# Who builds the transposed one-hot of a chunk: GpSimd in 16 pieces between its gathers, in place of VectorE in one operation

## What is computed

```python
edge_index_t = jnp.stack([src, dst], axis=1)
xn = _layernorm(x, axis=-1)
x = x + _L0_gnn_ref(xn, edge_index_t, ...) + _L0_mix_ref(xn[None], ...)[0]
x = x + _L0_ffn_ref(_layernorm(x, axis=-1)[None], ...)[0]
```

```python
qe = q[:, c, :]; ke = k[:, r, :]; ve = v[:, r, :]
sim = jnp.einsum('hed,hed->eh', qe, ke) * scale
m = jax.ops.segment_max(sim, c, num_segments=bs)
p = jnp.exp(sim - m[c])
s = jax.ops.segment_sum(p, c, num_segments=bs)
attn = p / s[c]
agg = jax.ops.segment_sum(out_e, c, num_segments=bs)   # out_e = attn * ve
```

## Time and profile before

| | |
|---|---|
| time, median of 3 runs | 1684.04 us (1683.97 to 1684.6) |
| profiled execution | 1672.81 us, span 1671.1 us |
| busy: TensorE, VectorE, ScalarE, GpSimd | 1051.0, 1016.4, 420.2, 573.4 us |
| attention rounds | from about 270 to 1293 us of the span |

### The profile page before, as it was taken

One profiled execution on the slowest core, in us unless ns is written; L12 is line 12 of the kernel. 1 busy time (PEld: TensorE's weight loads), 2 busy tenths in 40 slices (PEclk: granted clock), 3 DMA queues, 4 the chain that ended last, 5 costly groups with the idle time before them and its releaser, 6 DMA issues. The chain is left out here.

```text
span 1671.1 us, 20984 instructions
## 1 busy us (share of the span) xinstructions
PE 1051.0 (63%) x4059; PEld 682.8 (41%) x4060; DVE 1016.4 (61%) x2562; ACT 420.2 (25%) x1228; POOL 573.4 (34%) x651
## 2 busy tenths in 40 slices
PE   0389563655656565565665656655656870899996
PEld 0245341433334343343433333333433570557574
DVE  5369866766666566666666666666677740234343
ACT  1212252222222222222222222222223240121211
POOL 1224336233433333334444433433330007323231
PEclk9789776777776667777677766777677955899998
DMA  4531324244444444444444444444430234143420
GB/s 141 83 126 62 98 58 125 86 132 116 122 127 119 114 114 114 114 119 122 129 130 129 127 130 117 122 128 118 114 103 1 88 127 124 45 151 102 155 95 11
DMA packets 85034, 181.19 MB, mean 108 GB/s; under 512 B 13797, under 2 KB 49819, under 8 KB 84999
## 3 DMA queue, kind: packets, MB, share of 16 engines
q0 software_dynamic: 39744, 120.22, 26.0%
q1 hardware_dynamic: 45255, 60.56, 11.6%
HBM read 158.49 MB, written 24.89 MB: 110 GB/s over the span
## 5 line engine op out<-in xcount | busy, mean ns | idle before, releaser
L1104 PE MATMUL at_pa<-at_pv,at_hot 128*125 128x264 f32 x832 | 321.2, 532 | 226.8 <-DVE agg L978 152.1
L1104 PEld LDWEIGHTS at_pa<-at_pv,at_hot 128*125 128x125 f32 x832 | 193.1, 253 | 327.3 <-issue 250.6
L850 POOL DMA_INDIRECT slot<-kv_d,idx x192 | 184.0, 958 | 295.0 <-ACT idx L859 242.9
L1047 PE MATMUL at_pq<-q,at_hotT 125*128 x1248 | 234.3, 332 | 78.3 <-DVE at_prod L986 55.0
L850 POOL DMA_INDIRECT at_slot<-kv_d,idx x192 | 184.1, 959 | 289.4 <-ACT idx L859 237.0
L1047 PEld LDWEIGHTS at_pq<-q,at_hotT 125*128 125x128 bf16 x1248 | 143.3, 115 | 164.3 <-issue 110.0
L978 DVE TENSOR_TENSOR agg<-agg,at_pa 125x264 f32 x416 | 176.7, 425 | 37.0 <-remote 10.2
L1021 DVE TENSOR_TENSOR at_pv<-at_slot,at_pp 128x528 f32<-128x528 f32 x104 | 71.8, 701 | 125.0 <-remote 74.7
L1021 DVE TENSOR_TENSOR at_pv<-slot,at_pp 128x528 f32<-128x528 f32 x104 | 71.8, 701 | 118.8 <-remote 74.8
L907 DVE TENSOR_REDUCE at_sc<-at_prod 128x16 f32<-128x512 f32 x208 | 139.4, 671 | 0.0
L865 ACT ACTIVATE at_habs<-iota_w,nloc_e 128x125 f32<-128x125 f32 x416 | 131.1, 386 | 0.2 <-issue 0.2
(11 more groups left out here) (297 smaller groups left out, 1462.7 us busy)
## 6 DMA issues: line engine op xcount, KB each, us to landing
slot<-in_w SPq DMA_DIRECT2D x16, 1024.0 KB, 6.3
at_locrow<-loc_d SPq DMA_DIRECT2D x26, 500.0 KB
slots_d<-slot SPq DMA_DIRECT2D x7, 516.0 KB
kv_d<-vst SPq DMA_DIRECT2D x25, 128.9 KB
base<-in_x SPq DMA_DIRECT2D x5, 625.0 KB
kv_d<-kst SPq DMA_DIRECT2D x25, 125.0 KB
x_d<-base SPq DMA_DIRECT2D x5, 625.0 KB
out<-base SPq DMA_DIRECT2D x5, 625.0 KB
```

Of the source, the lines that this page charges most:

```text
L850: pool.indirect_dma_start(slot[par][:, u, :], None, m.kv_d, bass.IndirectOffsetOnAxis(ap=m.idx[:, par, u:u + 1].bitcast(U32), axis=0)).the ...
L1047: mm = pe.matmul(pq[j % 2][:, (u % 2) * D:(u % 2 + 1) * D], hotT[:, u, :], at(m.q3, window)[:, part, :], start=(part == 0), stop=(part == 2))
L1104: mm = pe.matmul(pa[u % 4][:, 0:H * VW], hot[:, u % 8, :], pv[:, u % 4, :, :].rearrange("p h c -> p (h c)"), start=True, stop=True)
```

## The change

VectorE's `turned_hots` is gone. GpSimd makes the same tile step by step, 125x128 each, with `turned_hot(u)`: all 16 steps ahead of the first loop for chunks 0 and 1; in the loop four steps (AHEAD) before the first gather of the chunk and then one behind each of the first 12 gathers. `hotT_made` now counts steps and no longer chunks, so SyncE waits for 16 times n, and TensorE waits once for each pair of steps and no longer once for a chunk.

```diff
@@ block.sync
-                        wait(sp, S.hotT_made, n)
+                        wait(sp, S.hotT_made, U * n)
@@ block.gpsimd
+                def turned_hot(u):
+                    pool.tensor_scalar(hotT[:, u, :], locrow[:, u * 128:(u + 1) * 128], m.iota_p[0:TT, 0:1], None,
+                                       ALU.is_equal).then_inc(S.hotT_made, 1)
+                pool.wait_ge(S.loc_in, 16)
+                for u in range(U):
+                    turned_hot(u)
                 gather_chunk(pool, m, 1, slot[1])
+                pool.wait_ge(S.loc_in, 32)
+                pool.wait_ge(S.q_spread, 8)
+                for u in range(U):
+                    turned_hot(u)
                 with pool.Fori(1, CH // 2) as k:
                     for par in range(2):
+                        pool.wait_ge(S.loc_in, 32 * k + 16 * par + 16)
+                        pool.nop(nofuse=True)
+                        pool.wait_ge(S.q_spread, 16 * k + 8 * par)
+                        pool.nop(nofuse=True)
+                        for u in range(AHEAD):
+                            turned_hot(u)
                         for u in range(U):
...
+                            if u + AHEAD < U:
+                                turned_hot(u + AHEAD)
@@ block.vector
-                def turned_hots(n):
-                    dve.wait_ge(S.loc_in, 16 * n + 16)
-                    wait(dve, S.q_spread, 8 * n)
-                    dve.tensor_scalar(flat(hotT[:, :, :]), locrow[:, :], m.iota_p[0:TT, 0:1], None, ALU.is_equal).then_inc(S.hotT_made, 1)
@@
-                        if nxt is not None:
-                            turned_hots(nxt)
@@
-                turned_hots(0)
                 dve.memset(m.agg.rearrange("p t h c -> p (t h c)"), 0.0).then_inc(S.at_const, 1)
@@ block.tensor
+                    if u % 2 == 0:
+                        pe.wait_ge(S.hotT_made, U * n + u + 2)
@@
-                        pe.wait_ge(S.hotT_made, nxt + 1)
@@
-                            if u == U - 2 * AHEAD:
-                                pe.wait_ge(S.hotT_made, nxt + 1)
@@
-                pe.wait_ge(S.hotT_made, 1)
```

## The result

In five runs beside the kernel before, the changed kernel took 1698.39 us (1693.38 to 1699.74) against 1684.04: ratio 1.0081, 95% interval 1.0064 to 1.0099, so 14 us slower. The forecast was 1556 us, faster.

What follows compares the result with a forecast made beforehand. The prediction took waiting on late TensorE signals during gathers to bound the round; 39.06 to 33.6 us over 24 rounds saves 130 us, the start adds 2, so 1684 - 128 = 1556 us, full range 1495 to 1765.

Steps and rivals of the forecast that it cites:

- What bounds the round, and the stall: Attention rounds of 39.06 us: late TensorE signals hold VectorE's eighth product to 20.23 us, 1.87 behind the twelfth gather.
- pauses on the transfer engines: Between gathers: a 1.60 us step leaves 0.34 us of pause behind each, expected to keep TensorE's signals in time.
- The piece, 0.33 us with ends 0.24 and 0.38: GpSimd's price for each 125x128 one-hot step, taken from an affine select; gathers would step by 1.60 us.
- The fetch is hidden: Target-row fetch after the sixteenth piece: there by 32 us, pieces by 33.5, before the next gather near 37; no cost.
- -0.66 us for VectorE's operation: Start of the round: removing VectorE's one-hot operation, taken to be on the path, saves 0.66 us a round.
- Landing 3.0 us behind the last gather, and 4.08 us from the last product to `fac`: End of the round: data land at 30.2 us; 4.08 less 0.66 later the next `fac` comes at 33.6.
- The start, +2 us: Before the first loop: pieces for chunks 0 and 1 delay the first product from 301.96 to near 304.
- TensorE's seven waits, nothing: Seven added TensorE waits a chunk cost nothing, as pieces come before the gathers and TensorE has 17 us to spare.
- pieces cost much: Rival, chance 0.10: stall gone but gathers step by 1.94 us, `fac` at 37.6, time 1651 us.
- Half and half: Rival, chance 0.09: signals still late in part, gain and longer gathers cancel out, about 1684 us.
- The moved stall: Rival, chance 0.12: VectorE stalls behind the eighth product until after the sixteenth gather; rounds of 45.3 us, 1834 us.
- a rule against the change: Elementwise work belongs on VectorE: 0.73 us a chunk there, against 5.2 us for 16 pieces on GpSimd.

Runs made afterwards that it cites:

- gap_ts: Kernel before plus an idle 125x125 comparison on GpSimd behind each of a chunk's first twelve gathers; 1634.2 us, ratio 0.973.
- base_c: Kernel before, unchanged, run again for its trace in a session without the stall; 1468.4 us.
- gap_128: Kernel before plus an idle 128x128 memset on GpSimd behind each of a chunk's first twelve gathers; 1682.9 us, ratio 1.001.
- late_fetch: Changed kernel with the target-row fetch held until all gathers of the chunk have landed; 1662.6 us, ratio 0.990.
- halves: Changed kernel, target row fetched half after the eighth piece, half after all gathers landed; 1641.4 us, ratio 1.119, session without the stall.
- gap_ts_last: gap_ts with the row fetch held until the tenth gather landed; 1670.0 us (1.136) without the stall; repeated with it as gap_ts_last_b, 1669.2 (0.992).
- gap_ts_loc_b: gap_ts with the row fetch held until the fourth group of indices is staged, session with the stall; 1636.8 us, ratio 0.972.

## Why the prediction was wrong, step by step

- **What bounds the round, and the stall** (8th product late because TensorE's signal is late while gathers follow each other): right for these sessions. gap_ts shows that more time between gathers is enough to remove it, base_c that without it the same program runs at 30.6 us a round with gathers and landings unchanged. That the late thing is a signal was an inference, and the records of raised semaphores bear it out (8.9 us late in the kernel before, 0.01 in base_c); why it is late stays open. That it comes 1.87 us behind the twelfth gather did not hold in gap_128. My note that pauses on the transfer engines would do it from 0.34 us on was not put to the test at that size: 0.20 (step 1.46) was too little, 0.60 was enough.
- **The piece, 0.33 us with ends 0.24 and 0.38**: this is the step that failed first. It took 0.63. I bounded it by a select and by half of a two-input sum, and none of these rows was a comparison with a scalar per partition. The sixteenth gather started at 29.5 us and not at 26.2: 3.3 us a round, 79 in all. The step of 1.87 lay inside my ends (1.36 to 1.94) only because I had allowed up to 0.30 us ahead of a piece, and it was 0.02.
- **The fetch is hidden**: wrong, and the second step that failed. Either of the two errors alone would have left the changed kernel faster than before: without this one it is at 1663 us (late_fetch), and without the 79 us of the pieces it would be near 1620, an estimate, if the stall stayed away. I asked only whether the row would be there for the pieces, and not what it would meet on its way. Late_fetch, halves and gap_ts_last bring it down to this: beside the middle gathers it is free, beside the last ones it holds back the data on which the round ends. Last product 35.8 us in the changed kernel, 33.3 in gap_ts: 2.5 us a round, 60 in all; VectorE's two rows of waits for gathered data come to 237 and 176 us, 61 apart. Of the 2.5 us, 1.6 come with the fetch alone (gap_ts_last), and the rest is not taken apart.
- **-0.66 us for VectorE's operation**: wrong. The earlier trace rows show 0.66 us between it and `sc_pen`, and `fac` behind that; but `fac` also waits for TensorE's chain, and comes 4.1 us behind the last product with the operation or without it. 16 us that were not there.
- **Landing 3.0 us behind the last gather, and 4.08 us from the last product to `fac`**: the second is right (4.1 everywhere), the first by luck. I took the end of the landing from the edge of a window, 779.40; the last packet landed at 778.96, 2.5 us behind the last gather, and 2.4 in gap_ts. I put nothing between the landing and the product, and there are 0.5 us. Together that makes the 2.9 of gap_ts.
- **The start, +2 us**: +6.4 between the two traces, though the first mark lies anywhere from 314.3 to 324.1 in traces of kernels that start as the one before; with pieces of 0.63 my own sum gives 16 x 0.30 = 4.8 more for the first chunk alone.
- **TensorE's seven waits, nothing**: right. In halves, where the fetch is out of the way, the round is that of the kernel without them.

The round adds up from there: 33.6 forecast, + 0.66 + 3.3 + 2.5 = 40.1, measured 39.9. For the profiled execution, 1545 + 24 x (39.86 - 33.6) + 4.4 for the start = 1700 us, measured 1699.3.

Of the rivals, "pieces cost much" was the nearest, with a price of 0.4 us where 0.63 came, and 1651 us without the fetch; halves measured 1641. "Half and half" named about the time, for a reason that didn't hold. The moved stall exists, at a step of 1.46 us, and costs as much as the stall itself (39.8 us a round), not the 45.3 that I read off the longest round.

The section on a rule against the change pointed the right way. The Trainium skill's advice to keep such work off GpSimd (GPSIMD Engine Reference, When to use GPSIMD, Engine selection) fits: 16 pieces cost GpSimd 10.0 us a chunk, for 0.73 on VectorE. The Trainium skill's figure of 1.03 cycles for an element (the same page, Performance versus the Vector engine) does not: 128 more columns cost 0.315 us in these rows, three times what it gives, and the measurement decides.

**Versions that beat both kernels**, in sessions with the stall, are gap_ts, 1634 us, and gap_ts_loc_b, 1637 (ratios 0.973 and 0.972), and by 1% late_fetch and gap_ts_last_b (0.990 and 0.992). All but late_fetch do it with work that is thrown away, and in a session without the stall the kernel before, 1467 us, beats all that I tried. Over both kinds of session the better kernel is the one before.

## What to carry to other kernels

When the price of the new operation decides, the nearest row must be of the same operation and width, or the range must hold a factor of two. A transfer that moves is to be followed to its new neighbours: what matters is which data it shares the wire with, and whether the path ends on them. And before one buys a stall off with work, one should run the kernel before in more than one session: this stall was a property of the session, worth an eighth of the time, and the cures cost 4 to 14% where there was nothing to cure.

## What the runs showed of the hardware that I had not expected

- One program takes 1467 us or 1680 us by session, on one chip too, with gathers of 0.96 us in both that land 2.5 us behind the last one. The difference is when the semaphore behind TensorE's products is raised while GpSimd issues gathers: 0.01 us after their end in base_c, 8.9 in the median of the kernel before. Traces from sessions with the stall also lack 7 to 36% of the records of raised semaphores.
- GpSimd's comparison of a bf16 row with a scalar per partition took 0.627 us for 128 columns and 0.942 for 256, and 0.632 for 125 columns from f32; a memset of 128x1 costs 0.12 us, of 128x128 0.22.
- A gather issued behind a GpSimd operation takes 1.02 us and starts 0.17 behind it; behind another gather it takes 0.96 and starts after 0.30.
- A 500 KB transfer cost 1.2 to 2.2 us of landing time beside the last gathers (gap_ts_last_b, changed kernel), and nothing beside gathers 7 to 9.
